# Attention scores from high and low halves of q and k, with the transposes of tile 3 moved into their own step

## What is computed

```
kv = (x @ w_kv_down) @ w_kv_up;  k, v = kv[..., :1024], kv[..., 1024:];  q = x @ w_q      # x: layernorm of the input
att = einsum('bqhd,bkhd->bhqk', q, k) * 64 ** -0.5
att = softmax(where(causal, att, -inf))
y = einsum('bhqk,bkhd->bqhd', att, v);  x = input + y @ w_out
```

## Time and profile before

| | |
|---|---|
| median of 3 runs | 962.83 us (962.78 to 963.06) |
| profiled execution, its own time | 964.63 us |
| its span, first to last instruction | 962.8 us |
| busy PE / DVE / ACT / POOL | 900.0 / 616.4 / 585.4 / 545.1 us |
| mean granted clock of TensorE | 0.98 of full speed |

### The profile page before, as it was taken

One profiled execution on the slowest core, in us unless ns is written; L12 is line 12 of the kernel. 1 busy time (PEld: TensorE's weight loads), 2 busy tenths in 40 slices (PEclk: granted clock), 3 DMA queues, 4 the chain that ended last, 5 costly groups with the idle time before them and its releaser, 6 DMA issues. The chain is left out here.

```text
span 962.8 us, 19642 instructions
## 1 busy us (share of the span) xinstructions
PE 900.0 (93%) x5614; PEld 619.0 (64%) x5615; DVE 616.4 (64%) x2375; ACT 585.4 (61%) x1483; POOL 545.1 (57%) x536
## 2 busy tenths in 40 slices
PE   3899999999999999999999999999852999999996
PEld 1566666666666666666666666666531888888885
DVE  2575677677767767776776677677744445544553
ACT  2677677667767766776676677667631444555453
POOL 2555554566466457646655764664553366656655
PEclk9999999999999999999999999999975999999999
DMA  6945330000000000000000000000001233333332
GB/s 198 332 178 232 139 87 1 7 13 17 1 13 20 4 7 12 18 1 12 21 3 7 12 18 1 12 20 5 3 31 34 31 47 49 46 44 47 44 44 28
DMA packets 43417, 44.32 MB, mean 46 GB/s; under 512 B 4288, under 2 KB 35904, under 8 KB 43216
## 3 DMA queue, kind: packets, MB, share of 16 engines
q0 software_dynamic: 16528, 26.03, 11.2%
q1 hardware_dynamic: 26816, 17.39, 6.5%
HBM read 15.28 MB, written 28.12 MB: 45 GB/s over the span
## 5 line engine op out<-in xcount | busy, mean ns | idle before, releaser
L318 POOL TENSOR_TENSOR prob<-prob,row_inv 128x512 f32<-128x512 f32 (+3 forms) x256 | 321.7, 1257 | 289.0 <-DVE row_inv L615 285.1
L445 ACT ACTIVATE prob<-prob,neg_max 128x256 f32<-128x256 f32 (+3 forms) x512 | 281.0, 551 | 171.3 <-DVE neg_max L608 171.3
L937 PE MATMUL low_ps<-PT,v_sb 128*64 128x512 f32 (+3 forms) x1024 | 153.6, 443 | 2.4 <-ACT PT L451 2.4
L405 POOL DMA_INDIRECT out<-prob,meta_row x71 | 111.0, 1563 | 35.1 <-issue 35.1
L937 PEld LDWEIGHTS low_ps<-PT,v_sb 128*64 128x64 f32 x1024 | 68.4, 137 | 94.8 <-issue 64.9
L926 PEld LDWEIGHTS low_ps<-ident,prob 128*128 128x128 f32 x768 | 86.5, 140 | 60.2 <-issue 50.1
L926 PE MATMUL low_ps<-ident,prob 128*128 128x128 f32 x768 | 108.4, 277 | 3.1 <-DVE neg_max L608 2.4
L821 DVE TENSOR_TENSOR prob<-mid_ps,prob 128x512 f32<-128x512 f32 x71 | 49.1, 692 | 84.1 <-ACT prob L541 52.7
L445 ACT ACTIVATION_READ_ACCUMULATOR prob<-prob,neg_max 128x1 f32 x512 | 96.7, 189 | 0.0
L608 DVE CUSTOM_DVE_ANT_0 prob<-mid_ps,mask 128x128 f32<-128x128 f32 (+1 forms) x256 | 93.5, 421 | 0.4 <-issue 0.2
L608 DVE CUSTOM_DVE_ANT_0 prob<-top_ps,mask 128x512 f32<-128x512 f32 x128 | 83.3, 689 | 12.3 <-PE low_ps L926 12.3
(11 more groups left out here) (168 smaller groups left out, 1699.7 us busy)
## 6 DMA issues: line engine op xcount, KB each, us to landing
routed_rows<-W_dn POOLq DMA_DIRECT2D x8, 2080.0 KB
routed<-routed_rows SPq DMA_DIRECT2D x71, 65.0 KB
X<-in_L_attn_x SPq DMA_DIRECT2D x8, 256.0 KB, 5.5
W_ffn<-in_L_ffn_Wg SPq DMA_DIRECT2D x8, 256.0 KB, 5.0
W_ffn<-in_L_ffn_Wu SPq DMA_DIRECT2D x8, 256.0 KB, 5.3
W_dn<-in_L_ffn_Wd SPq DMA_DIRECT2D x8, 256.0 KB, 4.5
out<-X SPq DMA_DIRECT2D x8, 256.0 KB, 2.3
out<-prob,meta_row POOLq DMA_INDIRECT x71
```

The source lines that it names most:

```text
L318: nc.gpsimd.tensor_tensor(p_pair(i), p_pair(i), row_inv[:, i, :].unsqueeze(2).to_broadcast([P, 2, P * (i + 1)]), ALU.mult).then_inc(S["nor ...
L405: nc.gpsimd.indirect_dma_start(out=out, out_offset=bass.IndirectOffsetOnAxis(ap=meta_row[:, q:q + 1], axis=0), in_=eo_sb[q], in_offset=Non ...
L445: nc.scalar.activation(p_at(i, h), p_at(i, h), ACT.Exp, bias=neg_max[:, i, h:h + 1], scale=-1.0, accum_out=row_sum[:, i, h:h + 1]).then_in ...
L937: last = nc.tensor.matmul(y_ps[h * HD:(h + 1) * HD, j * P:T], v_sb[:, half, j, o + h * HD:o + (h + 1) * HD], PT[:, h, j, j:NT, :].rearrang ...
```

## The change

- Scores: `qk_sb` holds a high part (ACT, `qk_hi`, one copy for q and one for k, rounded to F32R) and a low part (DVE, `qk_lo`, two subtractions). Each tile and head takes three F32R matmuls, high by high, high by low, low by high, in place of one float32 matmul.
- Order on PE: scores, `values(n - 1)`, `project(n + 1)`, transposes of tile 1, `project_out(n - 1)`, transposes of 2, `v_chunk`, transposes of 0 and 3. Tile 3 is transposed in its own step, and the values of a step come right behind the next step's scores. Transposed tile 2 lies in `low_ps` now and tile 3 in `top_ps`.
- ACT: all exps first, then `y_copy(n - 1)` (moved from DVE), `qk_hi(n + 1)`, `v_copy`, `t3_copy(n)`. DVE: `inv` of 2 before the pre and post work, `inv` of 3 before the copy of tile 1, `qk_lo(n + 1)` between the copies of tiles 1 and 2. POOL: the four norms in ORDER within their step, and the scatters of routed rows in three groups behind them.
- `xn_sb`, `xn2T` and a buffer of the experts share memory with `PT`, `outT` and `y_sb`.

```diff
@@ -76,10 +76,9 @@
...
-        qk_sb = sb("qk_sb", [P, 2, T])
+        qk_sb = sb("qk_sb", [P, 2, 2, T], F32R)
...
-        xn_sb = sb("xn_sb", [P, NT, C])
...
@@ -136,13 +134,17 @@
...
+        xn_sb = [PT[:, 0, j, i, :] for j, i in ((1, 0), (2, 0), (2, 1), (3, 0))]
+        xn2T = outT
...
-        hT_sb = [outT, xn2T]
+        hT_sb = [outT, y_sb]
...
@@ -163,7 +165,7 @@
...
-        SCATTER_EARLY, SCATTER_LATE = {7: 0, 8: 2, 1: 4}, {7: 1, 8: 3, 1: 5, 2: 6, 3: 7}
+        SCATTERS = {7: (0, 3), 8: (3, 6), 1: (6, 8)}
...
@@ -187,8 +189,8 @@
...
-            ps, o = {2: (top_ps, 0), 3: (low_ps, 0)}[i]
-            return ps[:, :].rearrange("p (h n) -> p h n", h=2)[:, :, o:o + w].rearrange("p h (j q) -> p h j q", q=P)
+            ps = {2: low_ps, 3: top_ps}[i]
+            return ps[:, :].rearrange("p (h n) -> p h n", h=2)[:, :, 0:w].rearrange("p h (j q) -> p h j q", q=P)
         def pt_sb(i):
...
@@ -357,21 +359,16 @@
             def step(n, k, pre=None, post=None, fills=False):
-                if n:
-                    norm(n - 1, 3)
...
-                if post is not None and k in SCATTER_EARLY:
-                    scatter_at(post, k, SCATTER_EARLY[k])
-                norm(n, 1)
+                for i in ORDER:
+                    norm(n, i)
...
-                norm(n, 0)
-                if post is not None and k in SCATTER_LATE:
-                    scatter_at(post, k, SCATTER_LATE[k])
-                norm(n, 2)
+                if post is not None and k in SCATTERS:
+                    scatter_at(post, k)
...
@@ -433,10 +429,16 @@
...
-            def qk_copy(n):
-                seen(act, S["qk_ready"], n + 1)
-                nc.scalar.activation(qk_sb[:, :, :].rearrange("p a n -> p (a n)"), mid_ps[:, :], ACT.Copy).then_inc(S["qk_copied"], 1)
+            def qk_hi(n):
+                for a in range(2):
+                    seen(act, S["qk_ready"], 2 * n + a + 1)
+                    nc.scalar.activation(qk_sb[:, 0, a, :], mid_ps[:, a * T:(a + 1) * T], ACT.Copy).then_inc(S["qkhi_done"], 1)
+            def y_copy(n):
+                seen(act, S["y_ready"], n + 1)
+                nc.scalar.activation(y_sb[:, :], y_ps, ACT.Copy).then_inc(S["y_copied"], 1)
             def exps(n, i):
@@ -455,28 +457,28 @@
...
-            def step(n, k, cur=True, prev=True, nxt=True, pre=None, post=None, v=True):
+            def step(n, k, cur=True, nxt=True, pre=None, post=None, v=True):
+                if cur:
+                    exps(n, 1)
+                    exps(n, 0)
...
                 if cur:
-                    exps(n, 1)
-                    exps(n, 0)
-                if prev:
-                    t3_copy(n - 1)
-                if cur:
...
+                    exps(n, 3)
+                y_copy(n - 1)
                 if nxt:
-                    qk_copy(n + 1)
-                if cur:
-                    exps(n, 3)
-                if v:
-                    v_copy(n + 3, (k + 3) % NP // NT, (k + 3) % NT)
+                    qk_hi(n + 1)
...
+                if v:
+                    v_copy(n + 3, (k + 3) % NP // NT, (k + 3) % NT)
...
+                if cur:
+                    t3_copy(n)
             def split_weights(k):
@@ -619,12 +622,14 @@
...
-            def y_copy(n):
-                seen(dve, S["y_ready"], n + 1)
-                nc.vector.tensor_copy(y_sb[:, :], y_ps).then_inc(S["y_copied"], 1)
-            def step(n, k, cur=True, prev=True, pre=None, post=None):
+            def qk_lo(n):
+                for a in range(2):
+                    seen(dve, S["qkhi_done"], 2 * n + a + 1)
+                    nc.vector.tensor_tensor(qk_sb[:, 1, a, :], mid_ps[:, a * T:(a + 1) * T], qk_sb[:, 0, a, :].bitcast(F32),
+                                            ALU.subtract).then_inc(S["qklo_done"], 1)
+            def step(n, k, cur=True, nxt=True, pre=None, post=None):
                 if cur:
...
@@ -632,6 +637,7 @@
...
+                    inv(n, 2)
...
@@ -649,14 +655,13 @@
...
                 if cur:
-                    inv(n, 2)
-                if prev:
-                    y_copy(n - 1)
+                    inv(n, 3)
+                    t_copy(n, 1)
+                if nxt:
+                    qk_lo(n + 1)
                 if cur:
-                    t_copy(n, 1)
-                    inv(n, 3)
+                    t_copy(n, 2)
...
-                    t_copy(n, 2)
             def split_weights(k):
@@ -747,17 +752,27 @@
...
-            step(0, 0, prev=False)
+            qk_lo(0)
+            for i in (1, 0, 2):
+                maxes(0, i)
+            inv(0, 1)
+            maxes(0, 3)
+            inv(0, 0)
+            inv(0, 2)
+            qk_lo(1)
+            inv(0, 3)
+            for i in (1, 2, 0):
+                t_copy(0, i)
...
-                step(NP * (B - 1) + k, k, post=B - 2)
+                step(NP * (B - 1) + k, k, nxt=k < NP - 1, post=B - 2)
...
-            step(STEPS, NP, cur=False)
+            step(STEPS, NP, cur=False, nxt=False)
...
@@ -870,66 +885,63 @@
...
-                    last = nc.tensor.transpose(post_ps[:, t * P:(t + 1) * P], xn_sb[:, t, :], ident[:, :])
+                    last = nc.tensor.transpose(post_ps[:, t * P:(t + 1) * P], xn_sb[t], ident[:, :])
...
             def project(n, pair, b):
-                seen(pe, S["xTlo_done"], b + 1)
+                if n == 0:
+                    pe.wait_ge(S["xTlo_done"], 1)
...
-                last.then_inc(S["qk_ready"], 1)
+                    last.then_inc(S["qk_ready"], 1)
             def v_chunk(n, b, half, t, bank=0):
-                seen(pe, S["xTlo_done"], b + 1)
+                if half == 0 and t == 0:
+                    seen(pe, S["xTlo_done"], b + 1)
...
             def scores(n, i):
                 if i == 1:
-                    seen(pe, S["qk_copied"], n + 1)
-                    seen(pe, S["t1_copied"], n)
-                    seen(pe, S["y_copied"], n - 1)
+                    seen(pe, S["qklo_done"], 2 if n == 0 else 0)
+                    seen(pe, S["t2_copied"], n)
                 if i == 0 and n:
...
                 if i == 3:
-                    seen(pe, S["t2_copied"], n)
-                for h in range(2):
-                    d = slice(h * HD, (h + 1) * HD)
-                    last = nc.tensor.matmul(scores_at(i, h), qk_sb[d, 0, i * P:(i + 1) * P], qk_sb[d, 1, 0:P * (i + 1)],
-                                            start=True, stop=True)
+                    seen(pe, S["t3_copied"], n)
+                for k, (a, b) in enumerate(((0, 0), (0, 1), (1, 0))):
+                    for h in range(2):
+                        d = slice(h * HD, (h + 1) * HD)
+                        last = nc.tensor.matmul(scores_at(i, h), qk_sb[d, a, 0, i * P:(i + 1) * P], qk_sb[d, b, 1, 0:P * (i + 1)],
+                                                start=(k == 0), stop=(k == 2))
...
-            def transposes(n, i, cur=True):
+            def transposes(n, i):
...
-                if i == 3 and cur:
-                    seen(pe, S["max_done"], 8 * (n + 1) + 2)
-                if i == 3 and not cur:
+                if i == 2:
...
-                    seen(pe, S["y_copied"], n)
-                if i == 1:
-                    seen(pe, S["t3_copied"], n)
                 if i == 0:
-                    seen(pe, S["qk_copied"], min(n + 2, STEPS))
+                    seen(pe, S["qklo_done"], 2 * min(n + 2, STEPS))
...
-                if i == 2:
-                    seen(pe, S["max_done"], 8 * n + 8)
...
-            def values(n, pair):
-                seen(pe, S["t3_copied"], n + 1)
-                for i in range(NT - 1):
+            def values(n, pair, cur):
+                if cur:
+                    seen(pe, S["max_done"], 8 * (n + 1) + 2)
+                for i in range(NT if not cur else 0):
...
@@ -944,23 +956,17 @@
...
-            def step(m, k, cur=True, prev=True, nxt=True, pre=None, post=None, v=True):
+            def step(m, k, cur=True, nxt=True, pre=None, post=None, v=True):
...
                 if cur:
                     for i in ORDER:
...
-                if prev:
-                    transposes(n - 1, 3, cur)
+                values(n - 1, (k - 1) % NP, cur)
...
                 if nxt:
...
-                if prev:
-                    values(n - 1, (k - 1) % NP)
-                if v:
-                    seen(pe, S["qk_copied"], n + 2)
-                    v_chunk(n + 3, m + (k + 3) // NP, (k + 3) % NP // NT, (k + 3) % NT)
                 if cur:
...
@@ -972,11 +978,15 @@
...
-                if prev:
-                    project_out(n - 1, (k - 1) % NP)
+                project_out(n - 1, (k - 1) % NP)
+                if cur:
+                    transposes(n, 2)
+                if v:
+                    seen(pe, S["qklo_done"], 2 * n + 3)
+                    v_chunk(n + 3, m + (k + 3) // NP, (k + 3) % NP // NT, (k + 3) % NT)
                 if cur:
...
-                    transposes(n, 2)
+                    transposes(n, 3)
```

(5 more changed lines are left out.)

18 lines of the change are left out of this document (9 added, 9 removed).

## The result

The changed kernel takes **987.87 us** (median of 4 runs, 985.95 to 989.25) against 962.84 for the kernel before: ratio 1.0258, 95% interval 1.0242 to 1.0274. It is 25 us slower, where 10 us faster was forecast; the profiled execution took 987.4 with a span of 985.6.

What follows compares the result with a forecast made beforehand. PE's own work was taken to bound the steady part. Steady steps -15.7, k = 5 +1.8, start +2.9, last sequence +1.4 and tail -0.5 gave -10.1 us on 962.8: 953 us, range 942 to 974.

Steps and rivals of the forecast that it cites:

- DVE's ledger: Ordinary step on DVE: up to 2.1 us of pre and post work ahead of tile 3's reciprocal costs nothing.
- Only k = 5 waits: In step k = 5, PE's ranks wait 0.3 us for DVE's choice; +1.8 us over six sequences.
- Scores: PE's scores in each step: three F32R passes take 2.09 us against 2.36; 0.29 less taken, period 9.99.
- narrow passes: Rival on tile 0's scores: narrow F32R passes run at float32 pace, 0.33 us a step, 974 us; chance 0.17.
- heads that don't overlap: Rival on PE's scores: the two heads don't run side by side in F32R, +1.9 us a step, about 1070; chance 0.05.
- the chain becomes the bound: Rival on hand-overs between engines: 0.6 us longer, a step loses 0.2 to 0.3 of its gain, 957 to 972; chance 0.13.
- Start: Step 0 into step 1: scores wait for tile 3's norm, step 1 starts at 38.9; net +2.9 us.
- Last sequence: Last sequence: DVE waits for ACT's split of weight blocks, maxes come late, 77.8 against 76.4 us; +1.4.
- with a v chunk 12.3: Last sequence, steps behind a weight split: T3 at 11.9, with a v chunk the step takes 12.3 us.
- Tail: After step 63: three weight blocks on ACT ahead of outT, done at 18.95 against 19.46 before; -0.5 us.
- Scatters: Grouped scatters on POOL end at 12.6 in the worst step, ahead of the next norm at 13.1.

Runs made afterwards that it cites:

- experiment 4: Experiment 1's kernel with unheld bn_stats dummies on DVE at the old place, ahead of tile 3's reciprocal: 960.77 us.
- experiment 1: On the changed kernel, DVE's pre and post work that stays in SBUF moved to the head of its step: 963.84 us.
- experiment 8: Experiment 1's kernel with the old float32 scores, one matmul per head and tile: 967.74 us.
- experiment 9: Changed kernel with three repairs (SBUF work, weight split, start): 947.66 us; then also `gap` behind the choice of experts and scatters as 2, 2, 2, 2: 940.90 us.

## Why the prediction was wrong

**The step that failed** is the one on DVE's ledger: "Pre and post work of up to 2.1 us on DVE now stands ahead of tile 3's reciprocal, at 4.4 to 6.5 at the latest; POOL reaches tile 3 at 6.5 anyhow". Its reasoning on the place was right (experiment 4); its duration was wrong. The 2.1 us were lengths of rows from a kernel in which POOL was mostly idle beside them. Beside the norms the work of k = 2 took 3.3, the reciprocal came at 7.7, and with it the norm of tile 3 and the copy of T1, for which PE idled 1.20 us; in k = 3 and 4 PE idled 0.52 and 0.81 us for the stretched rows themselves. So "Only k = 5 waits" was wrong for k = 2, 3, 4 and 6. Moving the work away gave 24.0 us (experiment 1) of the 35 between forecast and result. The forecast's terms for the steps from 1 to 56 (580.1 before, -15.7, +1.8, and -0.8 in step 1) come to about 565 us, and experiment 1 has 565.8. That they meet so closely is partly luck: k = 5 and 8 are 0.3 to 0.4 longer than the forecast has them, k = 3 and 4 0.2 shorter. The profile of before held the warning, in the minimum, median and maximum of a group, which the mean hides:

```profile
L731 DVE TENSOR_TENSOR picked<-chosen,pos x16: 178/184/535, 177.1 to 725.7; 128x32 f32<-128x32 f32 x16
```

The same operation takes 178 or 535 ns; the long ones end 0.05 us behind a norm of 614 ns beside them. I took means.

**Scores**: right in the mechanism. They take 2.12 against 2.09, and an ordinary step 9.96 against 9.99. The step's number is partly luck: the scores give 0.24 of it (experiment 8), not 0.29, and the new order, which the forecast let change nothing, another 0.08 (10.28 to 10.20 with the old scores). The forecast's own sum gave 0.27 (2.36 to 2.09) and took 0.29 without a reason. The chances of narrow passes (0.17) and of heads that don't overlap (0.05) went to cases that the runs exclude; "the chain becomes the bound" had the direction, through PE waiting in the extra steps and not in the ordinary ones, but with 957 to 972 about a third of the size.

**k = 5**: +0.3 forecast, 11.67 against 11.0 without a wait, so +0.6, of which 0.5 was `gap`, held up by a norm and standing ahead of the choice (experiment 9).

**Start**: step 1 at 40.66 for 38.9. I had the wait for the norm of tile 3, not that DVE's copy of T1 is queued behind its reciprocal, for which PE idled 2.53 us.

**Last sequence**: +7.3 for +1.4. The step of DVE idling for ACT's split was right (first max late by 2.5), but "with a v chunk 12.3" left out that `values(n - 1)` wait for tile 1's maxes, 1.9 us on PE, and in two of the three steps then run at the lower clock: 13.6, 13.8 and 13.2. **Tail**: outT at 18.8 behind step 63, forecast 18.95; behind that copy the kernel takes 254.1 where it took 251.6, and no run was made for those 2.5 us alone; other profiled runs have 250.5 to 255.1 there, so they may be no more than the spread between runs.

**Scatters**: "end at 12.6 in the worst step, ahead of the next norm at 13.1" was right about the norm and missed DVE's max in front of it (last section), worth 0.4 us a sequence (experiment 9).

## What to carry to other kernels

Before work on DVE is moved, write down what POOL does at the new place. A row's length belongs to its neighbours as well as to its operation, so look at its minimum and maximum and find the neighbour that ends with the long ones. Then check two-sidedly, as here: stretched work taken away from the place, and unstretched work of the same length put there.
